# First layer's offsets: the convolution copied to memory by ScalarE behind the roots, roots by halves, one drop moved

## The reference, cut to what matters

```
x1  = depthwise 3x3 convolution of x with dw_w, + dw_b
x1  = layernorm over the 64 channels (eps 1e-5), * ln_g + ln_b
x1  = gelu(x1)
off, mask = x1 @ w_off + b_off,  x1 @ w_mask + b_mask     (72 + 36 columns)
```

## Time and profile before

| What | Value |
|---|---|
| median of 3 runs | 1407.38 us (1406.61 to 1409.52) |
| the profiled execution, own time | 1405.99 us |
| its span, first to last instruction | 1404.2 us |
| PE matmul busy | 1119.7 us (80%) |
| DVE busy | 986.8 us (70%) |
| POOL busy | 701.7 us (50%) |
| ACT busy | 635.9 us (45%) |
| `offsets0`, first matmul to last `widest` | 25.68 to 109.98 us |

### The profile page before, as it was taken

The page is one execution under the profiler, slowest core; times in us unless marked ns, Lnnn a source line. Parts: engine busy times, 40 slices in busy tenths (PEclk is TensorE's granted clock), DMA queues, the critical chain, the costliest instruction groups (busy, mean ns, idle before and its releaser), DMA issues. The chain is left out here.

```text
span 1404.2 us, 32323 instructions
## 1 busy us (share of the span) xinstructions
PE 1119.7 (80%) x13632; PEld 574.4 (41%) x13632; DVE 986.8 (70%) x1209; ACT 635.9 (45%) x1082; POOL 701.7 (50%) x550
## 2 busy tenths in 40 slices
PE   2860059977849999999999767599999999998748
PEld 1430057753315555555555434133333333334313
DVE  3678955666978888888888566946666666667623
ACT  1444024443636666566666527034444444445410
POOL 2001012103347777767777403068888888888600
PEclk9985579998959999999999978889999999999859
DMA  4100000002201111111111004000000000002002
GB/s 84 22 1 0 0 2 3 2 3 48 53 29 30 30 30 31 43 30 30 30 30 35 12 0 116 20 1 2 2 2 2 1 1 2 1 2 77 2 18 69
DMA packets 28885, 31.40 MB, mean 22 GB/s; under 512 B 19149, under 2 KB 21774, under 8 KB 27966
## 3 DMA queue, kind: packets, MB, share of 16 engines
q1 hardware_dynamic: 28573, 28.96, 7.9%
q10 hardware_dynamic: 160, 0.30, 0.1%
HBM read 20.91 MB, written 5.35 MB: 19 GB/s over the span
## 5 line engine op out<-in xcount | busy, mean ns | idle before, releaser
L2121 POOL TENSOR_TENSOR arena_sb<-arena_sb 128x768 f32<-128x768 f32 x168 | 322.4, 1919 | 121.1 <-ACT arena_sb L2082 100.5
L2082 ACT ACTIVATE arena_sb<-ps 128x768 f32<-128x768 f32 x216 | 174.8, 810 | 242.7 <-PE ps L2011 240.5
L2136 DVE TENSOR_REDUCE arena_sb<-ps 128x4 f32<-128x1536 f32 x108 | 188.2, 1756 | 128.9 <-PE ps L1978 128.4
L1615 DVE TENSOR_TENSOR arena_sb<-ps,arena_sb 120x768 f32<-120x768 f32 x216 | 206.8, 957 | 11.0 <-DVE arena_sb L1610 0.6
L2011 PE MATMUL ps<-arena_sb 33*64 33x384 f32 x1728 | 187.5, 502 | 11.4 <-ACT arena_sb L2082 5.5
L1643 POOL TENSOR_SCALAR xp_sb<-xp_sb 128x384 f32<-128x384 f32 x92 | 137.3, 1492 | 98.2 <-ACT xp_sb L1555 89.0
L1513 PE MATMUL ps<-arena_sb 120*64 120x216 f32 x1536 | 182.1, 359 | 0.0
L2023 PE MATMUL ps<-arena_sb 64*64 64x384 f32 x1728 | 168.1, 488 | 3.4 <-ACT arena_sb L2089 3.4
L1497 PE MATMUL ps<-xn_sb,arena_sb 32*120 32x384 f16 x1728 | 120.9, 354 | 11.4 <-DVE xn_sb L1604 4.3
L1570 ACT ACTIVATE xp_sb<-ps 128x432 f32<-128x432 f32 x192 | 101.8, 530 | 61.0 <-PE ps L1513 60.9
L1610 DVE COPY arena_sb<-ps 120x384 f32<-120x384 f32 x216 | 118.5, 549 | 4.6 <-PE ps L1497 3.4
(11 more groups left out here) (239 smaller groups left out, 1530.4 us busy)
## 6 DMA issues: line engine op xcount, KB each, us to landing
arena_sb<-pixel_major SPq DMA_DIRECT2D x96, 120.0 KB, 2.3
pixel_major<-arena_sb SPq DMA_DIRECT2D x24, 108.0 KB
x_sb<-in_x SPq DMA_DIRECT2D x4, 576.0 KB, 8.5
arena_sb<-arena_sb SPq DMA_DIRECT2D x8, 288.0 KB, 5.5
xn_sb<-in_W SPq DMA_DIRECT2D x1, 2304.0 KB, 9.3
arena_sb<-in_W SPq DMA_DIRECT2D x1, 2304.0 KB, 8.3
out_x<-x_sb SPq DMA_DIRECT2D x24, 96.0 KB, 2.2
arena_sb<-arena_sb SPq DMA_DIRECT2D x24, 1.5 KB
```

The lines of the kernel that those rows point to most:

```text
L1615: v_.tensor_tensor(bmat[m % 2][:, 2 * CH * t:2 * CH * t + 2 * CH].rearrange("p (e n) -> p e n", e=2), p_y[t % 2], xs[t % 2].rearrange("p ( ...
L2082: act.activation(pt[g % SLOTS].rearrange("p (h n) -> p h n", h=2), p_scores(g), ACT.Exp)\
L2121: pool.tensor_tensor(acc, first, pt[g % SLOTS], ALU.add).then_inc(S["pool_added"], 1)
L2136: v.tensor_reduce(part.rearrange("p (a u j) -> p a u j", a=3, u=NB)[:, a, :, jc], p_m(m), AX.X, ALU.max)\
```

## The change

It does four things. ScalarE takes the roots half by half, each with its own wait and signal, and TensorE signals the variance half by half. ScalarE then copies the convolution plus `cb` from PSUM into `z` (Identity, both halves, signal `copied`). VectorE multiplies that copy with the reciprocal, both operands in SBUF, where it read PSUM and added `cb` itself; taps wait for `copied` rather than for `z`. VectorE's drop of the last pair's half 0 moves from before the first reciprocal to behind it.

```
--- before.py
+++ after.py
@@ -294,7 +294,7 @@
     sq, inv, z, gel = (big[:, 2 * CH * i:2 * CH * i + 2 * CH].rearrange("p (h n) -> p h n", h=2) for i in range(4))
     cb = k["small"][:, 2:3]
     S = {n: signal(k, "off0_" + n) for n in
-         ("bias_ps", "bias", "conv_ps", "sq", "var_ps", "root", "inv", "z", "gelu", "om_ps", "om", "top", "loaded")}
+         ("bias_ps", "bias", "conv_ps", "sq", "var_ps", "root", "copied", "inv", "z", "gelu", "om_ps", "om", "top", "loaded")}
 
     def pair(at):
         return ps[:, at:at + 1024].rearrange("p (h n) -> p h n", h=2)[:, :, 0:CH]
@@ -312,7 +312,7 @@
             def taps(n, which):
                 b2, i = divmod(n, NP)
                 if which[0] == 0 and n >= 2:
-                    pe.wait_ge(S["z"], 2 * (n - 1))
+                    pe.wait_ge(S["copied"], n - 1)
                 for t in which:
                     dy, dx = divmod(t, 3)
                     for h in range(2):
@@ -327,11 +327,11 @@
 
             def variance(n):
                 pe.wait_ge(S["sq"], n + 1)
-                if n:
-                    pe.wait_ge(S["root"], n)
                 for h in range(2):
-                    mm = pe.matmul(p_var[:, h, :], k["halfm"][:, :], sq[:, h, :], start=True, stop=True)
-                mm.then_inc(S["var_ps"], 1)
+                    if n:
+                        pe.wait_ge(S["root"], 2 * n + h - 1)
+                    pe.matmul(p_var[:, h, :], k["halfm"][:, :], sq[:, h, :], start=True, stop=True)\
+                        .then_inc(S["var_ps"], 1)
 
             def offsets(n, h):
                 pe.wait_ge(S["gelu"], 2 * n + h + 1)
@@ -368,12 +368,16 @@
                 b2, i = divmod(n, NP)
                 act.wait_ge(S["conv_ps"], n + 1)
                 if n:
-                    act.wait_ge(S["var_ps"], n)
+                    act.wait_ge(S["var_ps"], 2 * n)
                 act.activation(sq, p_conv[n % 2], ACT.Square, bias=cb).then_inc(S["sq"], 1)
-                act.wait_ge(S["var_ps"], n + 1)
+                for h in range(2):
+                    act.wait_ge(S["var_ps"], 2 * n + h + 1)
+                    if n:
+                        act.wait_ge(S["z"], 2 * n + h - 1)
+                    act.activation(inv[:, h, :], p_var[:, h, :], ACT.Sqrt, bias=k["eps"][:, 0:1]).then_inc(S["root"], 1)
                 if n:
-                    act.wait_ge(S["z"], 2 * n)
-                act.activation(inv, p_var, ACT.Sqrt, bias=k["eps"][:, 0:1]).then_inc(S["root"], 1)
+                    act.wait_ge(S["gelu"], 2 * n)
+                act.activation(z, p_conv[n % 2], ACT.Identity, bias=cb).then_inc(S["copied"], 1)
                 for h in range(2):
                     act.wait_ge(S["z"], 2 * n + h + 1)
                     if n:
@@ -398,16 +402,14 @@
             v.tensor_tensor(cb, vec[:, VC["dw_b"]:VC["dw_b"] + 1], ps[:, 2048:2049], ALU.subtract).then_inc(S["bias"], 1)
             v.wait_ge(S["bias"], 1)
             for n in range(PAIRS):
-                if n:
-                    offsets(n - 1, 0)
-                v.wait_ge(S["root"], n + 1)
                 for h in range(2):
+                    v.wait_ge(S["root"], 2 * n + h + 1)
                     v.reciprocal(inv[:, h, :], inv[:, h, :]).then_inc(S["inv"], 1)
-                    if n:
-                        v.wait_ge(S["gelu"], 2 * n + h - 1)
+                    if n and h == 0:
+                        offsets(n - 1, 0)
+                    v.wait_ge(S["copied"], n + 1)
                     v.wait_ge(S["inv"], 2 * n + h + 1)
-                    v.scalar_tensor_tensor(z[:, h, :], p_conv[n % 2][:, h, :], cb, inv[:, h, :], ALU.add, ALU.mult)\
-                        .then_inc(S["z"], 1)
+                    v.tensor_tensor(z[:, h, :], z[:, h, :], inv[:, h, :], ALU.mult).then_inc(S["z"], 1)
                 if n:
                     offsets(n - 1, 1)
                     widest(n - 1, 0)
```

## The result

The changed kernel takes 1401.11 us (median of 5 runs, 1399.38 to 1401.55); the kernel before took 1407.38 us beside it (median of 5, 1405.71 to 1409.52). The ratio is 0.995, with a 95% interval of 0.9939 to 0.9962. The prediction was 1401.9 us in a range of 1399.0 to 1405.2. In a second comparison the changed kernel took 1401.87 us, ratio 0.9949 (0.9936 to 0.9963).

What follows compares the result with a forecast made beforehand. The prediction took a loop of waits, TensorE close behind, as the bound: pairs of 10.59 instead of 11.47 us bring the last drop but two from 101.11 to 95.58, gain 5.5; 1407.38 - 5.5 = 1401.9 us, range 1399.0 to 1405.2.

Steps and rivals of the forecast that it cites:

- The bound: Middle pairs of the offsets stage: a loop of waits of 11.46 us, with the drop standing between root and reciprocal.
- Half-root: ScalarE's root over one half, unseen in the trace: taken at 0.58 us, with bounds 0.45 and 0.90.
- R: Start of a pair's first half-root on ScalarE, put 2.27 us behind Square's start, through the table load.
- Rival 4: ScalarE: a table load blocks longer than its record, so no gain; 1408.3 or 1408.8 us; chance 0.03.
- Product from memory: VectorE's product with both operands in SBUF: taken at 0.55 us, where the form it replaces takes 0.62.
- the taps' wait on the copy: TensorE's wait ahead of the taps: satisfied long before TensorE gets there, so the 1.09 us stall goes.
- Loop B: Loop of waits through TensorE's one offsets buffer, taps 5 to 8 and Square: 10.59 us a pair, the longest.
- loop A: Loop of waits through z, with both reciprocals and products, Gelu and Square: 10.48 us a pair.
- The tail: End of the stage, a chain of offsets matmuls, drops and largest values: matmuls left at 2.50 us twice.
- Rival 1: End of the stage: TensorE keeps the higher clock, 2.3 us more, gain 7.8, 1399.6 us; chance 0.10.
- Rival 2: TensorE bounds more than counted, its stream broken by the buffer wait: gain 3.9, 1403.5 us; chance 0.10.
- Loop C: Loop of waits through TensorE's queue of offsets matmuls, taps and variance: 10.41 us a pair.

## Why the prediction was right, point by point

- **The bound.** The drop between root and reciprocal was part of it: undone, 0.96 us a pair comes back. It was not all of it, as the moved drop alone shows.
- **Half-root.** Taken at 0.58; it takes 0.57 to 0.58. The other bounds (0.45, 0.90) were far off. The table load, not the variance, sets R, as counted: the load at 65.97 ends at 67.25, R is 67.27. I had added 0.09 behind the load; it is 0.02 here. The Trainium skill's page "ScalarE: Activation LUTs", section What ACT_TABLE_LOAD costs, adds a drain of about 1.38 us; the changed kernel, where the root waits for nothing but the load, shows none. Rival 4 falls with it.
- **Product from memory.** Taken at 0.55; it takes 0.55 to 0.56, with GpSimd at 0.00 in the stretch. This agrees with the Trainium skill's page "VectorE: DVE Perf Modes", section Two Vector instructions with no wait between them, by which VectorE reads a second SBUF tensor through an interface shared with GpSimd. No run here has GpSimd busy beside this product.
- **The copy.** Free, as said, and nearly useless, which was not said. The step that failed is "the taps' wait on the copy ... so the 1.09 us stall goes": with the wait on z put back, the stall stays away. The half-root and the moved drop, which bring z 1.3 us earlier, remove it.
- **The loops.** Loop B was forecast as the longest, 10.59 against 10.48 and 10.41, and it is, at 10.39 against 10.28 for loop A. Each is about 0.20 too long for much the same terms: root to reciprocal 0.03 rather than 0.11 (I had taken the first pair's delay), Square to root 2.21 to 2.22 rather than 2.27, the drop 0.77 rather than 0.83 (0.69 to the product rather than 0.75).
- **The sum.** Four middle steps 0.2 too long make 0.8. The first variance matmul came at 35.64 in the profiled execution, 0.71 later than before, which nothing in the change causes: with the same instructions up to there it came at 35.01 with the copy made twice and at 36.19 in the second execution. The two errors cancel by luck: forecast 95.58 for the last drop but two, 95.42 measured. TensorE's weight loads at the start of the stage, first of the changed kernel, then of the kernel before:

```profile
29.61 0.24 PEld L322 LDWEIGHTS ps<-arena_sb 64*64 64x64 f32 x4 [0.40 <-issue]
30.25 0.20 PEld L322 LDWEIGHTS ps<-arena_sb 64*64 64x64 f32 x4 [0.40 <-issue]
30.63 0.14 PEld L322 LDWEIGHTS ps<-arena_sb 64*64 64x64 f32 x4 [0.19 <-issue]
```

```profile
28.79 0.25 PEld L322 LDWEIGHTS ps<-arena_sb 64*64 64x64 f32 x4 [0.39 <-issue]
29.26 0.14 PEld L322 LDWEIGHTS ps<-arena_sb 64*64 64x64 f32 x4 [0.22 <-issue]
29.59 0.14 PEld L322 LDWEIGHTS ps<-arena_sb 64*64 64x64 f32 x4 [0.18 <-issue]
```

  The distance of two loads falls from 0.64 to 0.33 us, in the changed kernel after 30.25, before after 28.79. Each 0.64 costs 0.3: two more of them and loads that begin 0.18 later make about the 0.71. The granted clock reads 1.00 over the whole stretch in both, so why the first loads are slower is not shown. So the change's own gain is 6.4 us in the stage, 0.9 more than forecast, and the medians say 6.3.
- **The tail.** Left at 2.50 twice, and so it was: matmuls of 2.50 at 96.39 above. The ones before them, at 92.06, also ran at the lower level, which they had not before; they have time to spare there. Rival 1 did not come with this change; with own buffers for the last pair the last matmuls did keep the higher level.
- **Rival 2.** Loop C with the taps as the rows show them separately would have been 10.70; they run in 4.10 us together, as counted by groups. The stall at the buffer is 0.26, where "about half a us" stood.
- **Behind the stage** nothing was forecast, and 1292.4 against 1291.6 lies within what unchanged instructions vary by.

## What to carry to other kernels

Write the loops of waits down, all of them, with every single-buffer wait and every in-order queue in one of them. The time per round is the longest. Two waits that stand side by side give little when either goes (0.12 and 0.20 us a pair here) and all when both go (1.08), so an edit should be tried together with the one that shields it. And look at the last round by itself: what double-buffers the loop has no more use there, and lending its memory to the tail brought another 4.4 us of the stage here, two thirds of what the whole change had brought, up to 1.1 of it by the clock.

## What the runs showed of the hardware that was not expected

- The same idle time of TensorE, 2.67 us, left the granted clock at 1.00 in one execution and lowered it to 0.77 over a window of 4 us in another, where 16 matmul records took 2.46 us and not 1.54. Behind an idle time of 2.61 us in the last pair the offsets matmuls ran at 0.50 in the changed kernel and at 1.00 in the kernel with own buffers for the last pair and in the one with a second product.
- In this stage ScalarE starts an activation 0.01 to 0.02 us after a table load ends, where the earlier trace rows have 0.09. VectorE, already waiting, starts 0.03 after ScalarE's result in the pairs behind the first and 0.11 after it in the first.
- Time spent in some 1290 us of unchanged instructions varied by 6.6 us over the fourteen profiled executions, as much as the whole gain, and by 4.4 us between two executions of one kernel. The stretch within the stage repeated to 0.02 us in both kernels that were profiled twice.
